# The second batch's distances moved into the opening, and item 0's scores put ahead of the next key, in a fused cross-attention and MLP block

## The reference

```python
q = ln(queries); kv = ln(tokens)
qp, kp, vp = q @ Wq.T + bq, kv @ Wk.T + bk, kv @ Wv.T + bv
scores = einsum('bhld,bhtd->bhlt', qh, kh) / sqrt(32)
dist = sqrt(sum((query_coords[:, :, None] - token_coords[:, None]) ** 2, -1))
scores = scores - spatial_scale[h] * dist + spatial_offset[h]      # masked tokens: -inf
attn = softmax(scores)
x = queries + (attn @ vh) @ Wo.T + bo
x = x + gelu(ln(x) @ W1.T + b1) @ W2.T + b2
```

## Time and profile before

| | us |
|---|---|
| median of 3 runs | 1207.32 |
| lowest and highest | 1204.98, 1208.12 |
| the profiled execution | 1204.9 |
| its span, first to last instruction | 1203.0 |
| PE busy | 1181.3 (98%) |
| POOL busy | 953.5 (79%) |
| DVE busy | 912.4 (76%) |
| ACT busy | 863.4 (72%) |

### The profile page before, as it was taken

How to read it: one execution, slowest core, us unless ns; L and a number is a source line. 1 busy time by engine, 2 the same in 40 slices (tenths; PEclk the granted TensorE clock), 3 DMA queues, 4 the chain that set the end, 5 groups by cost and what they waited for, 6 DMA issues and landing times.

```text
span 1203.0 us, 27763 instructions
## 1 busy us (share of the span) xinstructions
PE 1181.3 (98%) x9632; PEld 806.3 (67%) x9632; DVE 912.4 (76%) x2482; ACT 863.4 (72%) x1964; POOL 953.5 (79%) x1198
## 2 busy tenths in 40 slices
PE   7899999999999999999999999999999999999999
PEld 4566666666676766667676666667666666766666
DVE  7987768787787978877797888778787877668322
ACT  5798787858677786867778786877778587757232
POOL 6889989788897988789798878889887887758321
PEclk9999999999999999999999999999999999999999
DMA  9776768989799898979989998889989797978553
GB/s 264 202 190 182 183 181 184 208 190 234 164 232 200 186 215 191 217 180 229 189 189 226 188 217 168 212 203 217 216 181 217 188 218 160 187 169 173 148 152 103
DMA packets 434524, 233.22 MB, mean 194 GB/s; under 512 B 349888, under 2 KB 374864, under 8 KB 434384
## 3 DMA queue, kind: packets, MB, share of 16 engines
q1 hardware_dynamic: 434384, 231.45, 83.7%
HBM read 109.66 MB, written 12.58 MB: 102 GB/s over the span
## 4 chain that ended last, share of the span: by engine, by line
PE 90%; ACT 4%; DVE 3%; DMA 1%; issue 1%; SPq 1%; DVEq 0%; ACTq 0%
PE ps_up L920 26%; PE ps_down L940 26%; PE ps_qk L821 13%; PE ps_vo L843 6%; PE ps_s L864 4%; PE ps_pv L846 3%; PE ps_pv L905 3%; PE ps_vo L846 3%; ACT soft L1111 1%; PE ps_down L968 1%; DVE soft L1441 1%; PE ps_down L876 1%; DMA w<-x_scratch 0%; ACT pT_whole L1124 0%; DMA w_stage<-in_w_qkv 0%
## 5 line engine op out<-in xcount | busy, mean ns | idle before, releaser
L920 PE MATMUL ps_up<-hT,w 128*128 128x256 f16 x3072 | 377.0, 273 | 0.0
L1111 ACT ACTIVATE soft<-soft,neg_max 128x256 f32<-128x256 f32 x512 | 255.6, 500 | 163.1 <-DVE neg_max L1441 161.8
L1441 DVE CUSTOM_DVE_ANT_0 soft<-ps_s,soft,factor 128x256 f32<-128x256 f32 x506 | 223.2, 477 | 188.8 <-PE ps_s L864 188.6
L940 PE MATMUL ps_down<-w,hid 128*128 128x512 f16 x1476 | 359.6, 378 | 0.8 <-ACT pT_whole L1124 0.6
L920 PEld LDWEIGHTS ps_up<-hT,w 128*128 128x128 f16 x3072 | 300.6, 98 | 85.9
L1683 POOL TENSOR_SCALAR p_nat<-soft,row_inv 128x256 f16<-128x256 f32 x448 | 265.9, 604 | 71.5 <-DVE row_inv L1454 67.8
L1692 POOL TENSOR_SCALAR soft<-dist,scale_neg,offset 128x512 f32<-128x512 f32 x256 | 271.4, 1060 | 17.3 <-DVE p_nat L1460 15.5
L1460 DVE SCALAR_TENSOR_TENSOR p_nat<-soft,row_inv,p_nat 128x256 f16<-128x256 f32 x448 | 268.5, 639 | 0.8 <-POOL p_nat L1683 0.8
L1164 ACT ACTIVATE u<-ps_up,bias,up_scale 128x256 f32<-128x256 f32 x256 | 142.5, 557 | 126.2 <-PE ps_up L920 123.4
L940 PEld LDWEIGHTS ps_down<-w,hid 128*128 128x128 f16 x1476 | 141.5, 97 | 127.0 <-issue 2.9
L1700 POOL TENSOR_SCALAR hid<-u,hid_scale 128x1024 f16<-128x1024 f32 x63 | 72.9, 1157 | 46.5 <-ACT u L1170 46.5
(11 more groups left out here) (180 smaller groups left out, 1549.2 us busy)
## 6 DMA issues: line engine op xcount, KB each, us to landing
w<-x_scratch SPq DMA_DIRECT2D x252, 256.0 KB, 3.1
stack<-qk_parts SPq DMA_DIRECT2D x256, 96.0 KB
raw<-in_ctx SPq DMA_DIRECT2D x32, 256.0 KB, 3.5
raw<-in_x SPq DMA_DIRECT2D x32, 256.0 KB, 4.2
c_stage<-in_w SPq DMA_DIRECT2D x16, 512.0 KB, 5.0
x<-in_x SPq DMA_DIRECT2D x32, 256.0 KB, 3.5
out<-x SPq DMA_DIRECT2D x31, 256.0 KB, 3.4
tok_rows<-in_tok_xy SPq DMA_DIRECT2D x16, 256.0 KB, 3.6
```

Of the source, the lines that this page charges most:

```text
L920: mm = e.matmul(ps_up[s % 2][:, 0:L], w_1_sb[:, wp, k, m * P:(m + 1) * P], hT[:, b % 2, :, xp * KT + k, :], start=(k, wp, xp) == (0, 0, 0) ...
L940: mm = e.matmul(ps_down[tt][:], left, w_2_sb[:, s % W2_RING, wp, :], start=first, stop=last)
L1111: e.activation(soft[:, ring, lc, :], soft[:, ring, lc, :], ACT.Exp, scale=-1.0, bias=neg_max[:, ring, lc:lc + 1], accum_out=row_sum[:, rin ...
L1441: e.tensor_tensor_reduce(soft[:, ring, lc, :], score_bank(i)[:, lc * T:(lc + 1) * T], soft[:, ring, lc, :], factor[:, 0:1], 3.0e38, ALU.ad ...
```

## The change

Five edits, all of order or place:

1. Group 1's key is projected in slot −1, behind `scores(0)`, and no longer in slot −2 ahead of it; its query in slot 1 and not 0; group 2's key in slot 2 and not 1. ACT's and DVE's parts and SP's copies follow one and two slots behind as before. Group 1's upper parts on ACT come ahead of the slot's exp.
2. The second batch's distances: an own load, issued by ACT, into an own tile; squares in slots −6 and −4, sum and root in slot −2 (before: squares 7 and 8, sum 9, root 10). The third batch's root moves from slot 18 to 25. Squares take the coordinates with scale −1 and the positive column as bias, so DVE's negation goes.
3. The upper parts of the rest of W_q are made by ACT in slot −3 and no longer by POOL in slots −21 and −2. DVE's lower parts of W_q's rest: pieces 0 and 1 in slot 0 right behind `score_max(0)` (before: slot −3), pieces 2 and 3 in slot 1 (before: 0). Of W_k's rest one piece is made ahead of the lower part of group 0's query, and three behind (before: two and two).
4. The total and norm of W_v: PE's product right behind `scores(0)` (before: slot −3), DVE's part behind `score_max(0)`, the root on POOL in slot −1.
5. `h_lo` follows the lower parts of W_1 and W_2 on DVE.

```diff
-        TOTAL = (-30, -28, -3, 0, 2, 5, 9, 13, 17, 20, 23, 26)
-        NORM = (-27, -24, -2, 1, 3, 6, 10, 14, 18, 21, 24, 27)
+        TOTAL = (-30, -28, -1, 0, 2, 5, 9, 13, 17, 20, 23, 26)
+        NORM = (-27, -24, 0, 1, 3, 6, 10, 14, 18, 21, 24, 27)
...
-        def qk_at(slot, first):
-            yield from (G for G in due(slot, first, GROUP, N_HG) if G != 1)
-            if slot == first + GROUP + 1:
-                yield 1
+        QK_OPENING = {(1, 0): -1, (1, 1): 1, (2, 0): 2}
+        def qk_at(slot, which, by):
+            yield from (G for G in due(slot, QK_PROJ + 2 * which + by, GROUP, N_HG) if (G, which) not in QK_OPENING)
+            yield from (G for (G, of), at_slot in QK_OPENING.items() if (of, at_slot + by) == (which, slot))
...
-                for G in qk_at(slot, QK_PROJ + 4):
+                for G in qk_at(slot, 1, 2):
                     stack_copies(G)
...
                 if -1 <= slot < UP:
                     scores(slot + 1)
+                if slot == TOTAL_V:
+                    total(AT[SEC_V])
...
+            def query_hi_rest():
+                gate.wait_ge(s_gs, GAINED_Q)
+                for k in range(KT):
+                    e.activation(w_sec[SEC_Q][:, HI, k, P:D], w_stage[SEC_Q][:, k, P:D], ACT.Copy, scale=gain[:, SEC_Q, k:k + 1]).then_inc(s_rhi_q)
+
             def dist_square(b, c):
-                gate.wait_ge(s_xy, DMA * (b + 1))
-                gate.wait_ge(s_cst, 1)
+                gate.wait_ge(*((s_xy_second, DMA) if b == 1 else (s_xy, DMA * max(b, 1))))
+                gate.wait_ge(s_small, 3 * DMA)
...
-                    e.activation(dst, tok_rows[:, c, :], ACT.Square, bias=q_neg[:, col:col + 1]).then_inc(s_sq)
+                    e.activation(dst, tok_of(b)[:, c, :], ACT.Square, scale=-1.0, bias=q_cols[:, col:col + 1]).then_inc(s_sq)
+
+            def load_second():
+                e.dma_start(tok_second[:], tok_xy[1:2].to_broadcast([P, 2, T])).then_inc(s_xy_second, DMA)
...
+                if slot == -26:
+                    load_second()
+                if slot == -6:
+                    dist_square(1, 0)
                 if slot == -4:
+                    dist_square(1, 1)
                     dist_sqrt(0)
+                if slot == -3:
+                    query_hi_rest()
+                if slot == -2:
+                    dist_sqrt(1)
...
-                for b in after_first(slot, 2, 10):
+                for b in after_first(slot, 2, 25):
                     dist_sqrt(b)
...
+                if slot == NORM_V:
+                    square_norm(AT[SEC_V])
+                    weight_lo_rest(SEC_Q, range(2))
...
-                if slot == -26:
-                    small_negate()
...
-                for sec, pieces, at_slot in ((SEC_K, range(2), -6), (SEC_K, range(2, KT), -4), (SEC_Q, range(2), -3), (SEC_Q, range(2, KT), 0)):
+                for sec, pieces, at_slot in ((SEC_K, range(1), -6), (SEC_K, range(1, KT), -4), (SEC_Q, range(2, KT), 1)):
...
-                for sec, pieces, at_slot in ((SEC_K, range(KT), -23), (SEC_Q, range(2), -21), (SEC_Q, range(2, KT), -2)):
-                    if slot == at_slot:
-                        weight_hi_rest(sec, pieces)
+                if slot == -23:
+                    key_hi_rest()
                 if slot == -22:
                     dist_sum(0)
-                for b in after_first(slot, 1, 9):
+                if slot == -2:
+                    dist_sum(1)
+                for b in after_first(slot, 1):
                     dist_sum(b)
```

More of the change, by code:

```diff
@@ L443, in at_pair, with after_first, tok_of, sq_of @@
                     yield b + len(early), which
[L445 to L450, removed]
+        def after_first(slot, steady, *third):
+            if slot in third:
+                yield 2
+            for b in due(slot, steady + BATCH * (1 + len(third)), BATCH, B - 2 - len(third)):
+                yield b + 2 + len(third)
+        def tok_of(b):
+            return tok_second if b == 1 else tok_rows
+        def sq_of(b):
+            return sq_second if b == 1 else sq
         def x_parts(b, n):
@@ L691, in sync_program @@
                     load_tile(b, n)
-                for b in after_first(slot, -3, 1):
+                for b in after_first(slot, -3):
                     load_coordinates(b)
@@ L995, in tensor_program @@
                 for which in range(2):
-                    for G in qk_at(slot, QK_PROJ + 2 * which):
+                    for G in qk_at(slot, which, 0):
                         for _ in range(STEPS):
@@ L999, in tensor_program @@
                 for w in range(N_W):
-                    if slot == TOTAL[w]:
+                    if slot == TOTAL[w] and w != AT[SEC_V]:
                         total(w)
@@ L1185, in scalar_program @@
                 for which in range(2):
-                    for G in qk_at(slot, QK_PROJ + 2 * which + 1):
-                        if not 0 <= slot < UP:
+                    for G in qk_at(slot, which, 1):
+                        if G == 1 or not 0 <= slot < UP:
                             qk_hi(G, which)
@@ L1196, in scalar_program @@
                 for which in range(2):
-                    for G in qk_at(slot, QK_PROJ + 2 * which + 1):
-                        if 0 <= slot < UP:
+                    for G in qk_at(slot, which, 1):
+                        if G != 1 and 0 <= slot < UP:
                             qk_hi(G, which)
@@ L1224, in scalar_program @@
                         dist_square(0, c)
[L1225 removed]
+                    for b in after_first(slot, -1 + c):
                         dist_square(b, c)
@@ L1537, in vector_program @@
                         diagonal(w)
-                    if slot == NORM[w]:
+                    if slot == NORM[w] and w != AT[SEC_V]:
                         square_norm(w)
@@ L1591, in vector_program @@
                     x_lo(b, n)
-                for b, tt in of_batch(slot, behind(H_APPLY, 1)):
-                    h_lo(b, tt)
                 for step in due(slot, 5, ITEM, MT):
@@ L1597, in vector_program @@
                     w2_lo(s)
+                for b, tt in of_batch(slot, behind(H_APPLY, 1)):
+                    h_lo(b, tt)
                 for which in range(2):
-                    for G in qk_at(slot, QK_PROJ + 2 * which + 1):
+                    for G in qk_at(slot, which, 1):
                         if 0 <= slot < UP:
```

37 lines of the change are left out of this document (21 added, 16 removed).

## The result

| | before | after |
|---|---|---|
| median of 20 runs each, taken side by side | 1204.99 | 1208.87 |
| lowest and highest, but for one run of after | 1203.99, 1208.12 | 1206.00, 1211.90 |
| the profiled execution, its span | 1204.9, 1203.0 | 1207.75, 1205.8 |
| mean granted clock over the whole, mean of the runs (before: of its 102 runs beside the experiments) | 0.9970 | 0.9942 |

A forecast was written before the change was run, and what follows sets the result against it. TensorE was taken as the bound, busy 1181.3 of 1203.0 us. An opening loss of 1.9 less 0.42 and 0.84 gave +0.6 us: 1207.9 us from the median of 1207.32, with a range of 1203.0 to 1211.0.

The forecast's parts named there:

- Part 1: Opening, item 0's scores ahead of group 1's key: VectorE's first maxima at 26.3 us, 1.4 us earlier than before.
- Part 2: Opening, group 1's query a slot later: its stack copies delay item 4's scores to 42.7, item 6's to 50.7 us.
- landing estimate of 2.1 us: Opening, group 1's stack copies (96 KB each): time taken for one to land, 2.1 us, before item 4's scores.
- opening's 1.9 us: Loss up to item 6's scores, 50.7 against 48.85 us; 1.1 and 2.9 with the bounds for the first maxima.
- rival (a): Opening, PE's clock halves in the new gap: 1209.6 us with one stretch (chance 0.17), 1211.3 with two (0.10).
- two-stretch case: Clock halved in two stretches of the opening's new gap, 1.7 us lost in each: 1211.3 us, chance 0.10.
- Part 3: Second batch's distances in the opening: first root delayed 0.2, first exp about 1 us later; load delays W_o at most 0.7.
- early bound of 25.5: Earliest start of VectorE's first maxima, 25.5 us, with item 0's bias tile started at 24.1 and 1.4 us long.
- late bound: Latest start of VectorE's first maxima, 27.3 us, with the new load's 0.7 us on top of copies at 26.4.
- Part 4: ScalarE relieved later: PE's waits at 77.03 and 105.14 us go, winning 0.42 and 0.84 us.
- Part 5: Negation and h_lo's order in slots 25 and 26: VectorE's slot 26 about 1 us shorter, PE not waiting, gain 0.
- Rival (c): Opening 1.2 us shorter and half clock behind 123.67 not returning: 1203.1 us, 1201.3 without the wait there; chance 0.12.

## Why the prediction was off in its size

**The bound and the method held.** Time lost ahead of item 6's scores arrives at the end, less what later waits give back: 5.34 − 2.65 against +2.8 in the span.

**Part 1 failed in two ways.** It asked when VectorE could begin item 0's maxima and named the copies as one of two things that come last. They came last, at 26.4; in the kernel before they had landed by 26.41, and no row shows when. They were issued at 23.33, not 0.7 earlier than the 22.61 of the kernel before but 0.7 later, since in this execution group 0's query projection ran at half clock (2.61 us at 19.45, 1.47 before). Others with the same order up to there issued them from 21.64 to 24.18, one at 23.48 at full clock, so the 0.7 is scatter as much as the change. First maxima 27.07, not 26.3: 0.8 us. The missing step is PE's side. The earlier trace rows show the key at 25.10 and the scores at 26.41 with no wait between, and I read it as the key delaying the scores. It filled PE's time while the copies flew, as the kernel with the key alone moved shows. Behind the scores the key and W_o's products stand ahead of item 1's scores: VectorE waited 1.61 us for them at 31.58, against a sum of its own instructions that had no wait in it. The key alone costs 1.2 us (0 to 2.4).

**Part 2 had the right mechanism.** Item 4's scores wait for the second group's copies, PE waits 2.46 us for group 2's key, item 6's have no wait; with the query back the first are released by maxima again and item 6's wait 1.14 us. The lower part was made at 40.11, not 38.2: 0.8 us from part 1 and 1.1 us from VectorE's slots 0 to 2, which took 13.0 us for my 11.9. The landing estimate of 2.1 us was good: the last of the four issues begins at 42.52, and 2.2 us later the scores start, as in four more executions. It isn't always so. With the root alone moved, the opening being that of the kernel before, item 4's scores waited for these copies too, 3.9 us behind their last issue at 35.98, with the DMA engines at a share of 0.86 until then (0.79 in the 2.2 us of the changed kernel):

```profile
39.90 0.39 PE L864 MATMUL ps_s<-stack 97*128 97x256 f16 x2 [2.15 <-DMA stack<-qk_parts]
```

So the kernel before had little slack here: its maxima and the landing of these copies were close to each other. The 8.02 us of PE's own work to item 6 took 9.44: half clock, 1.42 us. (At full clock it took 8.03 with the query back: 9.17 less the wait of 1.14.)

So the opening's 1.9 us became 1.9 + 0.8 + 1.1 + 0.1 + 1.4 = 5.3. This is the sum of one execution each; over the runs the loss of the whole is 3.1, and the terms aren't known to better than the scatter above. The last term is rival (a), and a part of the 1.1 is too. I gave this rival's two-stretch case 0.10, at 2 × 1.7 us. The argument against it, that waits of 1.77 and 1.15 us had brought no fall, was about shorter waits in a fuller stretch than those of 2.9 and 2.5 us that the change makes.

**Part 3.** The first root came at 24.89 and not by 23.55 (23.35 and the 0.2 that I allowed), as ScalarE waited 1.82 us for group 0's query projection ahead of the squares; with it item 0's bias tile, at 25.63, so that the early bound of 25.5 for the maxima was out of reach. The first exp came 3.3 us later (31.87, before 28.61) and not 1: ahead of it stands the key's upper part, for which ScalarE waited 1.59 us, until PE had projected the key at half clock. That the early distances are free was wrong by about what they gain, 0.6 us, if the estimate above holds. The rest of the change, 2.6 us (1.3 to 4.0) with all projections in their old places, I can't assign further: the W_q pieces' place and W_v's norm weren't tried alone, and part of it may be the clock. The Trainium skill's rule on issuers (DMA: Bandwidth & Descriptors, Issuing engines are not separate DMA queues), that transfers share the engines whoever issues them, is neither borne out nor contradicted: without the load the time is 0.8 us lower with overlapping intervals, and the 0.7 us that I counted by it in the late bound is no larger than that.

**Part 4 held and was too small.** The waits of 0.42 and 0.84 are gone, and each comes back (0.41, 0.84) when its cause is put back. Between items 10 and 26 1.50 us were won for my 1.26. Counted by the score matmuls, these waits stand in slots 13 and 21 (items 14 and 22) and not in the slots 10 and 19 of the prediction and the expectations, which are those of the roots or next to them; no time changes by it. Table loads are two fewer, as forecast: ahead of exp 71 and not 72, ahead of the root 15 and not 16.

**Part 5 was wrong at 0.** In the kernel before `h_lo` waits on VectorE for GpSimd, with the key's lower part and the next maxima behind it:

```profile
125.19 0.69 DVE L1422 TENSOR_TENSOR h_nat<-x_n,h_nat 128x512 f16<-128x512 f32 x1 [1.40 <-POOL h_nat L1662]
```

After, a lower part of W_1 or W_2 stands ahead of it, and its wait is 0.51 us (at 128.96). The order alone doesn't do that: with the root back in slot 18 the wait is 1.38 us again, but the slot takes 4.21 us and not 4.80. From item 27's to item 28's scores it is 3.96 us, where it was 4.80; the slot before shrank from 4.84 to 4.54. With part 4: 1.50 + 0.30 + 0.84 = 2.64, the whole later gain. I had taken the lack of a wait at 128.47 as proof that nothing was late. PE was slow there. With the root alone moved, PE is at full clock and does wait, and slot 26 takes 4.65 us:

```profile
122.79 0.38 PE L864 MATMUL ps_s<-stack 97*128 97x256 f16 x2 [1.40 <-DVE neg_max L1445]
...
127.44 0.38 PE L864 MATMUL ps_s<-stack 97*128 97x256 f16 x2 [1.32 <-DVE neg_max L1445]
```

So the half clock of the earlier trace rows that I priced at 1.7 us cost 4.80 − 4.65 = 0.15: it stretched work into a wait that would have been there. The maxima say the same: in both traces they begin 3.63 us behind item 27's scores (127.30, 126.42), and item 28's scores wait for them, so a faster PE wins no more than the 0.15. Rival (c) rested on that 1.7.

## What to carry to other kernels

Before moving work out of the way of a waiting instruction, ask what else that instruction waits for: work that is done while a transfer is under way costs nothing there, and is paid for where it goes. Of a producer moved a slot later, follow the chain through every engine with the waits in it, not one engine's instructions end to end; one execution doesn't settle what a small move costs there, as the same opening scattered by 0.7 us. Price a slow clock by the distance between two fixed points against an execution at full clock, not by the lengths of the slow matmuls.

## What the runs showed of the hardware

**The clock scatters within one kernel.** The kernel before, the same program, had mean clocks from 0.992 to 1.000 in 102 runs. Within kernels, over 257 runs, 0.001 less of mean clock goes with 0.52 us more (standard error 0.03). 0.001 of 1205 us is 1.2 us, so a little under half of what a busy PE would lose arrives; slot 26 shows one place where the rest goes, into a wait. By this slope 1.5 us of the change's 3.1 go with its lower clock (0.0028), an estimate, which doesn't say what lowered the clock.

**Half clock began in or behind waits of 1.4 to 4.4 us in the opening, but not each time.** The profiled execution of the kernel before has waits of 1.92 and 1.77 us with full clock behind them. The kernels before, with the root alone moved, and with root and `h_lo` moved have the same opening. In one profiled execution of each, the granted clock from 24 to 32 us was 1.00, 1.00 and 0.63. A single trace can't tell where an edit puts such a stretch; the mean clock over the runs can tell whether there are more of them.

**When the first copies land isn't set by when they are issued.** Issued at 20.81, 22.14, 23.33 and 24.18 us they released item 0's scores at 27.05, 27.22, 26.42 and 29.43; in five more executions 21.78, 22.66, 22.70, 22.89 and 23.48 gave 27.47, 26.54, 26.72, 28.97 and 28.72. The DMA engines are at a share of 1.01 to 1.05 from 20 to 24 us in the first four; which of the loads that are under way holds the copies up isn't known.
